# Graph attention layer: eight groups of edges of the fourth node block are gathered last

## The reference

```
a1 = jnp.exp(jax.nn.relu(e @ W_att_1 + b_att_1))        # e = [h[src], h[dst]]; a2, a3 alike
att1 = jax.ops.segment_sum(a1, dst, num_segments=N)
avg_a = (a1 / att1[dst] + a2 / att2[dst] + a3 / att3[dst]) / 3.0
m = avg_a * relu(relu(relu(hs @ W_msg_1 + b_msg_1) @ W_msg_2 + b_msg_2) @ W_msg_3 + b_msg_3)
h_neigh = jax.ops.segment_sum(m, dst, num_segments=N) / jnp.maximum(deg, 1.0)
out = jax.nn.relu(jnp.concatenate([h, h_neigh], axis=1) @ W_c1 + b_c1) @ W_c2 + b_c2
result = _layernorm(x + out)
```

## Time and profile before

| | us |
|---|---|
| median of the timed runs (3) | 1004.28 |
| lowest and highest | 1003.66, 1011.09 |
| span of the profiled execution | 776.9 |
| TensorE busy in it | 628.2 |
| VectorE busy | 583.1 |
| GpSimd busy | 569.0 |
| ScalarE busy | 425.4 |

### The profile page before, as it was taken

How to read it: one execution, slowest core, us unless ns; L and a number is a source line. 1 busy time by engine, 2 the same in 40 slices (tenths; PEclk the granted TensorE clock), 3 DMA queues, 4 the chain that set the end, 5 groups by cost and what they waited for, 6 DMA issues and landing times.

```text
span 776.9 us, 17471 instructions
## 1 busy us (share of the span) xinstructions
PE 628.2 (81%) x5157; PEld 513.5 (66%) x5157; DVE 583.1 (75%) x1947; ACT 425.4 (55%) x1055; POOL 569.0 (73%) x604
## 2 busy tenths in 40 slices
PE   9951989987978777988887888888888877778785
PEld 5741677755754556977777777777777766667674
DVE  4884577798888786677777777777787878787875
ACT  6566677787555435767677767673132233332323
POOL 7777777777777777777777777777777777777750
PEclk9985677799786775999999999999898999899796
DMA  7884333335743233333333333334434445444421
GB/s 232 252 209 102 79 77 87 77 80 72 82 81 77 66 97 78 83 83 79 80 81 78 81 78 82 77 83 106 100 94 118 104 104 138 101 108 104 100 49 34
DMA packets 83029, 75.66 MB, mean 97 GB/s; under 512 B 34904, under 2 KB 66432, under 8 KB 82928
## 3 DMA queue, kind: packets, MB, share of 16 engines
q0 software_dynamic: 19008, 39.82, 25.1%
q1 hardware_dynamic: 63632, 34.52, 16.1%
q10 hardware_dynamic: 288, 0.13, 0.1%
HBM read 64.88 MB, written 9.52 MB: 96 GB/s over the span
## 4 chain that ended last, share of the span: by engine, by line
DVE 37%; PE 26%; issue 15%; ACT 13%; DVEq 3%; POOL 2%; DMA 2%; SPq 1%; ACTq 0%
DVE fin L1741 9%; PE bank L1405 7%; ACT bank L1518 5%; DVE acc L1862 5%; PE bank L884 3%; DVE counts L1711 3%; DVE fin L975 3%; DVE work L1840 3%; PE bank L1428 2%; DVE fin L1698 2%; DVE side L1772 2%; PE bank L1411 2%; DVE work L1845 2%; ACT work L1539 2%; ACT work L1579 2%
## 5 line engine op out<-in xcount | busy, mean ns | idle before, releaser
L1227 POOL DMA_INDIRECT work<-message_table,src_t x554 | 527.9, 953 | 168.9 <-issue 166.1
L1405 PE MATMUL bank<-work 128*128 128x144 f32 (+8 forms) x1188 | 188.2, 313 | 56.6 <-DVE acc L1862 56.5
L1405 PEld LDWEIGHTS bank<-work 128*128 128x128 f32 x1188 | 172.5, 221 | 72.5 <-issue 71.9
L1579 ACT COPY work<-bank 128x192 f32<-128x192 f32 (+7 forms) x126 | 37.3, 296 | 186.1 <-DVE work L1814 173.1
L1445 PE MATMUL bank<-work,fin 128*128 128x129 f32 (+1 forms) x882 | 113.4, 284 | 0.0
L1862 DVE TENSOR_TENSOR acc<-acc,bank 128x192 f32 (+8 forms) x297 | 88.8, 299 | 32.7 <-issue 7.1
L1518 ACT ACTIVATE bank<-hot_logit 128x384 f32<-128x384 f32 (+1 forms) x147 | 72.7, 494 | 69.8 <-DVE fin L1741 60.3
L1445 PEld LDWEIGHTS bank<-work,fin 128*128 128x128 f32 (+1 forms) x882 | 104.3, 195 | 2.5 <-issue 0.6
L1845 DVE TENSOR_TENSOR work<-bank,work 128x576 f32<-128x576 f32 (+7 forms) x126 | 86.2, 684 | 13.1
L1741 DVE SCALAR_TENSOR_TENSOR fin<-bank,counts 128x384 f32<-128x384 f32 (+1 forms) x147 | 81.4, 554 | 17.8 <-ACT bank L1518 17.3
L1509 ACT ACTIVATE hot_logit<-logits_or_x,work 128x384 f32<-128x384 f32 (+1 forms) x147 | 88.3, 600 | 0.0
(11 more groups left out here) (152 smaller groups left out, 787.6 us busy)
## 6 DMA issues: line engine op xcount, KB each, us to landing
work<-message_table,src_t POOLq DMA_INDIRECT x554
side<-near_nodes SPq DMA_DIRECT2D x102, 48.0 KB
side<-logit_parts SPq DMA_DIRECT2D x297, 0.8 KB
message_table<-work SPq DMA_DIRECT2D x12, 262.0 KB, 4.0
work<-message_table SPq DMA_DIRECT2D x48, 65.5 KB
work<-in_x_t SPq DMA_DIRECT2D x12, 256.0 KB, 4.3
fin<-in_x SPq DMA_DIRECT2D x11, 256.0 KB
logits_or_x<-in_x_t SPq DMA_DIRECT2D x11, 256.0 KB, 3.4
```

What stands on the lines that cost most here:

```text
L1227: pool.indirect_dma_start(out=rows_of(n)[:, t, :], out_offset=None, in_=table[:, :], in_offset=bass.IndirectOffsetOnAxis(ap=src_t[:, h, g: ...
L1405: pe.matmul(sums[:, at:at + HEADS * w], rows_here[:, t, 0:P], wt_of(i)[:, t, :], start=h == 0, stop=h == TILES - 1)
```

## The change

The groups 100 to 107 belong to the fourth block of nodes (block 3, nodes 384 to 511). They are taken out of the long units and stand at the end of `first_order` as four short units, with windows 20 wide. There is one long unit less (22), and there are 127 units. Block 3 is left out of the first layer, which now has three blocks, and becomes the layer LAST. The blocks are cut into fifteen layers: three, ten times four, A (44, 45), B (46, 47), C (48) and LAST (3). B and C are fed by groups that come before the late ones; B starts six units ahead of the end and C four, and all their steps but C's 5 to 7 stand ahead of the last unit's sums.

```diff
+LATE_BLOCK, LATE_FROM, LATE_GROUPS = HOT, 100, 8
...
-    LONG = COUNT_STEPS
+    LONG = COUNT_STEPS - 1
     long_from = -(-n_hot // (2 * pair)) * 2 * pair
-    long_end = long_from + (LONG - 1) * 2 * pair
+    late_a, late_b = LATE_FROM, LATE_FROM + LATE_GROUPS
+    long_end = long_from + (LONG - 1) * 2 * pair + LATE_GROUPS
...
-    first_order += [tuple(range(g, g + 2 * pair)) for g in range(long_from, long_end, 2 * pair)]
+    first_order += [tuple(range(g, g + 2 * pair)) for g in range(long_from, long_end, 2 * pair)
+                    if not late_a <= g < late_b]
     first_order += [tuple(range(g, min(g + pair, n_groups))) for g in range(long_end, n_groups, pair)]
+    MAIN = len(first_order)
+    first_order += [tuple(range(g, g + pair)) for g in range(late_a, late_b, pair)]
...
-        sizes = [CHUNK] * (n_blocks // CHUNK - 1)
-        rest = n_blocks - sum(sizes) - 1
-        sizes += [rest - rest // 2, rest // 2, 1]
-        finals = [(sum(sizes[:c]), nb) for c, nb in enumerate(sizes)]
+        n_four = (n_blocks - LATE_BLOCK - 1) // CHUNK - 1
+        sizes = [LATE_BLOCK] + [CHUNK] * n_four
+        rest = n_blocks - 1 - sum(sizes)
+        sizes += [(rest - 1) // 2, rest // 2, 1]
+        finals = [(sum(sizes[:c]) + (c > 0), nb) for c, nb in enumerate(sizes)] + [(LATE_BLOCK, 1)]
...
-        final_at += [expected_end(A) + 1, expected_end(B) + 1]
+        final_at += [U - 9, U - 6, U - 4]
...
         final_tail = {
-            U - 4: [(B, 1), (A, 5)],
-            U - 3: [(B, 2), (A, 6)],
-            U - 2: [(B, 3), (A, 7)],
-            U - 1: [(C, 0), (B, 4), (LAST, 0), (LAST, 1), (C, 1), (LAST, 2), (B, 5), (C, 2), (LAST, 3), (LAST, 4),
-                    (C, 3), (LAST, 5), (B, 6), (C, 4), (B, 7), (C, 5), (LAST, 6), (C, 6), (LAST, 7), (C, 7)],
+            U - 4: [(B, 2), (A, 5), (C, 0), (C, 1)],
+            U - 3: [(B, 3), (C, 2), (A, 6), (B, 4), (B, 5), (B, 6)],
+            U - 2: [(C, 3), (A, 7), (B, 7), (C, 4)],
+            U - 1: [(LAST, 0), (LAST, 1), (C, 5), (LAST, 2), (C, 6), (LAST, 3), (C, 7), (LAST, 4), (LAST, 5), (LAST, 6),
+                    (LAST, 7)],
         }
...
-                node_limits[g] = least_node(i)
+                node_limits[g] = least_node(i) if i < MAIN else LATE_BLOCK * P
...
-                        n = min(REGS - g % REGS, end - g)
+                        n = min([REGS - g % REGS, end - g] + [a - g for a in (late_a, late_b) if a > g])
...
-                        chain(dve.tensor_reduce(late[:, :], limit[0:1, :], AX, ALU.max))
+                        most_late = float((LATE_BLOCK + 1) * P - width_of(late_a))
+                        chain(dve.tensor_scalar(late_limit[0:1, :], bank[SIDE_BANKS[0]][0:1, late_a:late_b], most_late, None,
+                                                ALU.is_gt))
+                        chain(dve.tensor_reduce(late[:, :], limits[0:1, :], AX, ALU.max))
```

More of the change, by code:

```diff
@@ L659, in gnn_program @@
         A, B, C = LAST - 3, LAST - 2, LAST - 1
+        assert sorted(i for b, nb in finals for i in range(b, b + nb)) == list(range(n_blocks))
         assert finals[LAST][1] == 1 and finals[B][1] <= LAST_FROM and finals[C][1] <= LAST_FROM
@@ L665, in expected_end @@
             most = share * n_edges + 6 * math.sqrt(share * (1 - share) * n_edges)
-            return min(len(first_order) - 1, sum(u[-1] < int(most / GROUP) for u in first_order))
+            return min(MAIN - 1, sum(u[-1] < int(most / GROUP) for u in first_order[:MAIN]))
         U = len(first_order)
@@ L716, in gnn_program @@
             for g in u:
-                node_limits[g] = least_node(i)
+                node_limits[g] = least_node(i) if i < MAIN else LATE_BLOCK * P
         limit_runs = [(a, len(list(run))) for a, run in itertools.groupby(node_limits)]
-        limit = mask[0:1, 1:THREE, :].rearrange("p j c -> p (j c)")[:, 0:n_groups]
-        assert n_groups <= (THREE - 1) * columns_most
+        n_limits = n_groups + LATE_GROUPS
+        limits = mask[0:1, 1:THREE, :].rearrange("p j c -> p (j c)")[:, 0:n_limits]
+        limit, late_limit = limits[:, 0:n_groups], limits[:, n_groups:n_limits]
+        assert n_limits <= (THREE - 1) * columns_most
         s_first = sem("s_first")
@@ L834, in gnn_program @@
         assert n_late * P <= TWO * hot_nodes
+        late_rows = []
+        for c in range(B, LAST + 1):
+            b, nb = finals[c]
+            whole, at = min(nb, n_nodes // P - b), late_at[c - B]
+            if whole > 0:
+                late_rows.append((x_late[:, at:at + whole, :],
+                                  x[b * P:(b + whole) * P, :].rearrange("(i p) f -> p i f", p=P)))
+            if whole < nb:
+                left = n_nodes - (b + whole) * P
+                late_rows.append((x_late[0:left, at + whole, :], x[(b + whole) * P:n_nodes, :]))
         def x_of(c):
@@ L845, in late_bias @@
             dve.wait_ge(s_wu, 32)
-            dve.wait_ge(s_xl, 32)
+            dve.wait_ge(s_xl, 16 * len(late_rows))
             here = x_late[:, 0:n_late, :]
@@ L1038, in load_late @@
             def load_late():
-                b = finals[B][0]
-                whole = n_nodes // P - b
-                left = n_nodes - (b + whole) * P
-                assert whole == n_late - 1
-                sp.dma_start(x_late[:, 0:whole, :], x[b * P:(b + whole) * P, :].rearrange(
-                    "(i p) f -> p i f", p=P)).then_inc(s_xl, 16)
-                sp.dma_start(x_late[0:left, whole, :], x[(b + whole) * P:n_nodes, :]).then_inc(s_xl, 16)
+                for to, of_x in late_rows:
+                    sp.dma_start(to, of_x).then_inc(s_xl, 16)
             def load_behind(c):
```

9 lines of the change are left out of this document (6 added, 3 removed).

## The result

| us | before | after |
|---|---|---|
| median of the timed runs on one chip (4 each) | 1005.57 | 1016.17 |
| lowest and highest | 1003.66, 1011.09 | 1014.57, 1020.08 |
| time of the profiled execution | | 1017.07 |
| its span | | 1013.1 |

The ratio is 1.0106, 95% interval 1.0061 to 1.0150: 10.6 us slower, where 4.1 were forecast, and 1016.2 lies above the range that ended at 1013.0.

The account below looks back on a forecast made before the run. VectorE's list, gaps included, was taken as the path up to the last unit. +8.0 us up to there, +1.1 to the last sum and -5.0 to the end made +4.1 on 1004.28: 1008.4 us, range 1000.5 to 1013.0.

Parts of the forecast that it names:

- (c): Final layers ahead of the last unit: VectorE's final steps there grow from 74.4 to 81.0 us, +6.6 us.
- (h): From the last sum to the end: mainly LAST is left, 10.9 us for 15.9, -5.0 us.
- (f): B's steps 5 and 6 in one unit: VectorE has nothing to do during two ScalarE activations, +0.7 us.
- (d): Window widths: narrower in units near the end, a little wider from unit 24 on, together -0.5 us.
- paid in full: Up to the last unit: every instruction put on VectorE costs its whole time, including the additional 6.6 us.
- Rival 3: Units from 117 on: TensorE takes over at its low clock, some 2.5 us a unit, +14, 1018; chance 0.05.
- (g): Last unit's L1820 to its last sum: products queue behind C's step 4, 5.4 us for 4.26, +1.1 us.
- (a): One long unit becomes short where counting the hot edges shares the engines: -2.5 us, seen at unit 25.
- (b): Groups that left the long units need units: one more short unit in front of the last, +3.0 us.
- They lie outside the span and nothing here touches them: The 227.4 us between the 776.9 us span and the timed median of 1004.28, added unchanged.
- Rival 1: GpSimd's gathers bound the kernel, so the added final work is hidden: -6.4 us, 997.9; chance 0.07.
- Rival 4: A limit raises the flag and the whole second pass runs: hundreds of microseconds more; chance 0.01.

Follow-up runs that it names:

- e13: The changed kernel again, unedited, against the kernel before on a chip of 780: ratio 1.0134, 792.64 us against 781.64.
- e17: The changed kernel again, unedited, beside the kernel before on a chip of 1000: ratio 1.0062, 1030.81 us.
- e18: The kernel before again, unedited, with its own trace on a chip of 1000: 1020.86 us, ratio 0.9889.
- e5: The changed kernel again, unedited, against the kernel before: ratio 1.0096.
- e1: The kernel before again, unedited, with a profile of its own: ratio 0.9995.
- e9: The changed kernel with 36 additional TensorE products that nothing reads, at five waiting places near the end, against the kernel before: ratio 1.0072.
- e4: The changed kernel with C's step 4 put behind the last unit's products on TensorE, against the kernel before: ratio 1.0029.
- e2: The kernel before with one long unit fewer (127 units) and nothing else, against the kernel before: ratio 0.9974.
- e14: The kernel before with 16 additional products in front of the last two units' products on TensorE, against the kernel before: ratio 1.0007.
- e6: The changed kernel with B's and C's final steps put back where the kernel before has them, against the kernel before: ratio 1.0028.
- e16: The changed kernel with B's and C's final steps put back, run once more on a chip of 780, against the kernel before: ratio 1.0011, 783.21 us.
- e8: The changed kernel with a slot of its own for C's scaled sums, all steps left in place, against the kernel before: ratio 1.0108.
- e15: The changed kernel with C's own slot and the additional TensorE products that nothing reads, against the kernel before: ratio 1.0072.

## Why the prediction was wrong

Its direction held, its size didn't. The comparison is from the row part of the seventeenth-last unit to the end, where the prediction's (c) to (h) give +3.6. On the chips of 780: 99.9 us (e13) for 92.9 (before), +7.0. On one chip of 1000: 105.8 (e17, with the clock at 1.00 in the step to the last unit) for 101.4 (e18), +4.4; after and e5 have 108.7 and 105.3, e1 100.3. Windows of that stretch up to the last unit's row part, split at the third-last's, in before, e13 and e9 (two rows each); us, busy us (instructions) of PE, PEld, DVE, ACT, POOL, then PEclk, DMA share, GB/s:

```profile
684.00:746.65 62.65, 51.04 (x432) 43.95 (x433) 50.45 (x178) 20.61 (x67) 47.41 (x51) 0.89 0.41 99
746.65:756.75 10.10, 7.72 (x73) 6.60 (x73) 8.07 (x35) 1.98 (x9) 4.38 (x5) 0.95 0.23 52
683.11:749.49 66.38, 52.19 (x438) 44.51 (x438) 53.29 (x201) 21.29 (x71) 50.22 (x54) 0.89 0.43 101
749.49:765.65 16.16, 13.79 (x91) 12.35 (x89) 8.78 (x42) 3.30 (x13) 2.49 (x3) 0.61 0.16 37
685.40:751.31 65.91, 54.22 (x474) 47.18 (x473) 53.29 (x201) 21.32 (x71) 50.05 (x53) 0.95 0.42 100
751.31:764.18 12.87, 12.01 (x121) 11.31 (x121) 8.93 (x42) 3.31 (x13) 3.12 (x4) 1.00 0.22 50
```

- **(c) to (f), up to the last unit: this is the step that failed.** It charged VectorE's instructions and next to nothing for what VectorE waits: 0.7, term (f). Predicted +7.5; measured +9.8, 3.7 in the fourteen units up to the third-last and 6.1 in the last two. The size of (c) was right: the instructions of the final layers take VectorE 31.1 us in these stretches for 24.9, 6.2 more where the sum has 6.6. Its other work shrank by more than (d) allows, so that it is busy for only 3.5 us more (62.1 for 58.5). The other 6.2 us are idle time (20.5 for 14.2), 5.4 of them in the last two units. So "paid in full" was not the rule that decided here; waits were. The wait of (f) is there (0.69), and beside it two that the sum hasn't: C's step 2 and B's step 5, in the same unit as B's steps 3 and 4, which stand behind the products on TensorE. A row of before that the prediction didn't count had the first of them (VectorE's waits from 547.5 to 756.75; us in total, times, longest):

```profile
DVE fin L975 <- ACT fin L920: 2.5, 4, 0.9
```

- **Rival 3, TensorE's low clock**, had 0.05 and no term in the sum, and it makes most of this idle time. The last two units have 0.61 for 0.95 of before. With the clock at 1.00 there and the same final steps (e9) the whole stretch is +6.0 and the idle time 16.6: 3.9 of the 6.2 us are gone, and what is left lies below the predicted 7.5. e17, at 1.00 in the last step without an edit, is +5.8 over e18. The place was not the units from 117 on, as I had it, where the clock is 0.89 in both kernels, but the last three; that the rival's 1018 lies near 1016.2 is chance. The prediction had read 0.50 behind an idle TensorE in before, and the change puts more waits of TensorE there.
- **(g)** Predicted +1.1, measured +1.5 (5.8 for 4.3). In after the last unit's products start 2.85 us behind L1841, as the sum has it (998.67), and they take 2.2 us at 0.50 for the 1.4 of the sum. e4 takes C's step 4 away and gets 1.0 back.
- **(h)** Predicted -5.0 with a tail of 10.9; measured -4.3 with 11.6, at a clock of 0.50. e9 has 10.1, with the clock high at the last sum.
- **(a), (b)** Predicted +0.5. e2, which is these two alone, is -2.6 us (-7.0 to +1.7). The sign that I had named for (a) isn't there: from unit 1's to unit 25's row part it is 216.8 us in before, 219.9 in e14, 216.8 in e13 and 215.1 to 220.2 in six variants of the changed kernel on chips of 780, a spread wider than the 2.5 us of the term. The seventeenth-last unit comes at 683.1 (e13) for 684.0, and at 921.0 (e17) for 916.1; e1, which is the same kernel as e18, has 923.2, so single traces don't settle these terms.
- **"They lie outside the span and nothing here touches them"** was a false reading, and it didn't cause the error: the loss is 10.5 us or so on the chips of 780 too, where the sum was read.
- **Rival 1, the gathers**: wrong on either kind. In after the last gather ends at 946.5, 49 us ahead of the last unit's L1841; in e13 it ends at 752.6, where before had 752.25, and the last unit came at 765.65, where the forecast had 764.8. That the two times nearly agree is partly luck: the stretch cost 2.3 us more than its sum, and what lies ahead of it 1.4 less. **Rival 4**: no second pass.

So some 7 of the 10.6 us are shown by stretches. e6 and e16, which put the final steps of B and C back behind the last sum, bring the time to within 0.3% of before, on one chip 1.0011 [0.9985, 1.0037] for the changed kernel's 1.0134 [1.0102, 1.0166]: the moved steps are the cause of the loss. About 3.5 us of it are in no trace. In e13 the profiled execution was the fastest of six (786.96 us; median 792.64), so a trace of a typical one is lacking; in e17 and e18 the remainder lies ahead of the seventeenth-last unit (+5.0), where e2 finds none. The granted clock of the timed executions gives a hint. Over e13's six it is 0.872 in the mean, over the 29 of before on the same chip 0.887, and within the six it goes with the time: 795.83 us at 0.861, 786.96 at 0.886, the one with the trace. A typical execution of the changed kernel so runs at the low clock for longer than its trace shows; where, and whether this is the cause of the 3.5 us, stays open.

No version beats the kernel before. Of the idea, the late groups cost nothing that the timed runs can tell (intervals of e6 and e16: 0.2% less to 0.7% more), and work moved in front of the last unit does.

## What to carry to other kernels

When final work is moved in front of the last unit, cost the chain through every engine that it crosses, behind what is queued there, not the busy time on the bound engine alone; and, where the trace shows a low clock behind idle TensorE, charge TensorE's work there at the low clock's times. Two layers that share a slot wait for each other when their steps fall in one unit, but look at what stands behind that wait before it is priced. Before a sum is read from a trace, compare its span with the timed runs: here a gap of 227 us wasn't overhead, it was an execution on another kind of chip.

## What the runs showed that I had not expected

**Two kinds of chip.** On four chips the kernel before ran at 1006 to 1023 us, on two at 781 and 782. VectorE's busy times differ little (585.1 in after, 584.3 in e13), the gaps do. On the slower chips TensorE issues single products 1.4 us apart in places, with nothing named to wait for; it is idle in this way for 117 to 171 us in all in after, e1, e17 and e18, and for at most 1.5 us in before, e9 and e13. The timeline of TensorE in after:

```profile
510.68 0.18 PE L1375 MATMUL bank<-side 48*128 48x45 bf16 x1 [0.56 <-issue]
512.12 0.18 PE L1375 MATMUL bank<-side 48*128 48x45 bf16 x1 [1.26 <-issue]
513.54 0.36 PE L1463 MATMUL bank<-work,fin 128*128 128x129 f32 x1 [1.25 <-issue]
514.97 0.37 PE L1463 MATMUL bank<-work,fin 128*128 128x129 f32 x1 [1.07 <-issue]
```

GpSimd then waits for places in the ring. Its waits in after (us in total, times, longest), and behind them those of e13:

```profile
POOL work L1245 <- issue: 146.5, 468, 4.1
POOL work L1245 <- remote: 104.4, 51, 2.9
POOL work L1245 <- PE bank L1429: 94.5, 34, 9.2
```

```profile
POOL work L1245 <- issue: 166.5, 546, 0.3
...
POOL work L1245 <- PE bank L1429: 2.1, 7, 0.3
```

In after the last gather ends some 49 us before the last unit's logits are summed, in before 4.5 and in e13 13, so on the slower chips GpSimd can't bound the end. What slows the issue there was not found.

**A free chain is worth little.** Of VectorE's 3.49 us wait for the shared slot only 0.3 to 0.8 came back when the slot was given (e8 against e17, e15 against e9): the same products were what B's step 5 needed next. Of the rest, 2.3 us were the clock (3.49 to 1.17 in e17).
